# The second attention layer's scores as float32 products in two row halves, in place of float16 halves

## The reference, cut to what matters

```python
# layer 0: 8 channels for f and g
f = xf @ wf + bf;  g = xf @ wg + bg;  hh = xf @ wh + bh
s = einsum('bnk,bmk->bnm', g, f)
x = gamma * softmax(s, axis=-1) @ hh + x

# layer 1: 64 channels for q, k and v
q = x @ Wq + bq;  k = x @ Wk + bk;  v = x @ Wv + bv
energy = einsum('bic,bjc->bij', q, k)          # 4096 x 4096, contraction over 64 channels
attn = softmax(energy, axis=-1)
out = einsum('bmn,bmc->bnc', attn, v)          # summed over the softmax's ROW index m
x = gamma * out + x
```

## Time and profile before

| what | value |
|---|---|
| median of three runs | 5068.23 us |
| the profiled execution | 5049.6 us, span 5047.8 us |
| TensorE (PE) busy | 4836.0 us, 96% |
| VectorE (DVE) busy | 3533.9 us, 70% |
| ScalarE (ACT) busy | 2755.7 us, 55% |
| GpSimd (POOL) busy | 1831.4 us, 36% |
| score products of layer 1 (L468, L469) | 4096 records, 800.4 and 790.3 us busy |
| value products of layer 1 (L480) | 4096 records, 1095.2 us busy |
| maximum (L880), bias (L883) | 1024 each, 1251.2 and 219.2 us busy |
| projection of q and k (L541) | 128 records, 111.9 us busy |

### The profile page before, as it was taken

One profiled execution on the slowest core, in us unless ns is written; L12 is line 12 of the kernel. 1 busy time (PEld: TensorE's weight loads), 2 busy tenths in 40 slices (PEclk: granted clock), 3 DMA queues, 4 the chain that ended last, 5 costly groups with the idle time before them and its releaser, 6 DMA issues.

```text
span 5047.8 us, 75059 instructions
## 1 busy us (share of the span) xinstructions
PE 4836.0 (96%) x21608; PEld 1511.7 (30%) x21608; DVE 3533.9 (70%) x6722; ACT 2755.7 (55%) x3752; POOL 1831.4 (36%) x821
## 2 busy tenths in 40 slices
PE   7999999999999999999999999999999999999999
PEld 3224222242222422233222422224222242222422
DVE  6566876678765787558866588665885568866687
ACT  2555655556555565546655466554664546655465
POOL 2772017710177003760037600475005740067300
PEclk6998999989999899998989989998998989999899
DMA  0000000000000000000000000000000000000000
GB/s 26 1 9 17 0 8 1 9 17 0 9 1 9 17 0 9 1 9 17 0 10 1 18 9 0 9 1 24 2 0 10 1 26 0 0 9 3 24 0 8
DMA packets 13506, 40.03 MB, mean 8 GB/s; under 512 B 2620, under 2 KB 2620, under 8 KB 10812
## 3 DMA queue, kind: packets, MB, share of 16 engines
q1 hardware_dynamic: 13244, 36.78, 2.4%
HBM read 19.99 MB, written 8.39 MB: 6 GB/s over the span
## 4 chain that ended last, share of the span: by engine, by line
PE 61%; DVE 24%; issue 11%; ACT 2%; DVEq 1%; SPq 0%; ACTq 0%; DMA 0%
PE sum_banks L401 20%; DVE chunk_max L880 15%; PE score_banks L383 10%; PE sum_banks L366 9%; PE score_banks L468 5%; PE score_banks L469 4%; PE sum_banks L480 3%; PE sum_banks L417 3%; PE score_banks L541 2%; PE score_banks L340 2%; DVE tile_max L727 2%; DVE exp_bias L883 2%; ACT e_whole L659 1%; DVE inv_sum L862 1%; PE score_banks L325 1%
## 5 line engine op out<-in xcount | busy, mean ns | idle before, releaser
L727 DVE TENSOR_REDUCE tile_max<-sum_banks 128x1 f32<-128x512 f32 (+1 forms) x2128 | 1363.4, 686 | 914.3 <-PE sum_banks L366 914.1
L292 POOL TENSOR_TENSOR e_sum<-e_sum,e_whole 128x1024 f32<-128x1024 f32 x704 | 1655.4, 2351 | 429.7 <-ACT e_whole L600 409.2
L600 ACT ACTIVATE e_whole<-score_banks,no_bias 128x1024 f32<-128x1024 f32 x1024 | 1141.4, 1115 | 1105.2 <-PE score_banks L383 1103.1
L659 ACT ACTIVATE e_whole<-score_banks,exp_bias,down 128x1024 f32<-128x1024 f32 x1024 | 1233.3, 1204 | 764.7 <-DVE exp_bias L883 764.7
L880 DVE TENSOR_REDUCE chunk_max<-score_banks 128x1 f32<-128x1024 f32 x1024 | 1251.2, 1222 | 227.1 <-PE score_banks L469 212.9
L401 PE MATMUL sum_banks<-e_whole,proj 128*64 128x512 f32 x4096 | 1109.2, 627 | 27.0 <-DVE att L769 27.0
L480 PE MATMUL sum_banks<-e_whole,v_scaled 128*64 128x512 f32 x4096 | 1095.2, 617 | 6.6 <-DVE v_scaled L870 6.6
L289 POOL TENSOR_TENSOR e_sum<-e_whole 128x1024 f32<-128x1024 f32 x32 | 75.2, 2349 | 2231.3 <-ACT e_whole L600 2231.3
L468 PE MATMUL score_banks<-k_high,q_split 128*128 128x512 f16 x2048 | 800.4, 391 | 70.7 <-ACT e_whole L659 38.8
L469 PE MATMUL score_banks<-k_low,q_split 128*128 128x512 f16 x2048 | 790.3, 386 | 0.0
L366 PE MATMUL sum_banks<-f_tr,g_tr 72*128 72x512 bf16 x2128 | 693.2, 400 | 30.6 <-DVE tile_max L727 15.8
(11 more groups left out here) (100 smaller groups left out, 2074.3 us busy)
## 6 DMA issues: line engine op xcount, KB each, us to landing
x_in<-in_x_dram SPq DMA_DIRECT2D x19, 1024.0 KB, 4.9
out_dram<-x_mid SPq DMA_DIRECT2D x32, 256.0 KB, 2.2
k_high<-k_high SPq DMA_DIRECT2D x32, 128.0 KB, 2.2
k_low<-k_low SPq DMA_DIRECT2D x32, 128.0 KB, 2.2
gammas<-in_L_conv_gamma_dram SPq DMA_DIRECT2D x2, 0.5 KB
w<-in_L_conv_wg_dram SPq DMA_DIRECT2D x1, 2.0 KB
w<-in_L_conv_bg_dram SPq DMA_DIRECT2D x1, 0.0 KB
w<-in_L_conv_wf_dram SPq DMA_DIRECT2D x1, 2.0 KB
```

The costliest lines, as they stand in the source:

```text
L292: nc.gpsimd.tensor_tensor(acc, acc, e_whole[:, i % U0, :], ALU.add).then_inc(e_added, 1)
L600: nc.scalar.activation(e_whole[:, i % U0, :].rearrange("p (a n) -> p a n", a=2), score_banks[:, 2 * (i % 2):2 * (i % 2) + 2, :], ACT.Exp, ...
L659: nc.scalar.activation(e_whole[:, u, :].rearrange("p (a n) -> p a n", a=2), score_banks[:, 2 * (u % 2):2 * (u % 2) + 2, :], ACT.Exp, bias= ...
L727: nc.vector.reduce_max(tile_max[:, blk, j:j + 1], sum_banks[:, (2 + j % banks) % 4, :], AX_X).then_inc(a_used, 1)
```

## The change

The scores of layer 1 are computed from q and k in float32. `q2` holds q twice, on partitions 0 to 63 and 64 to 127. `k2` holds k's even blocks of 512 columns on partitions 0 to 63 and its odd blocks on 64 to 127. A step then has two products: the one of `h` 0 takes partitions 0 to 63 of both operands and writes one bank, the one of `h` 1 takes partitions 64 to 127 and writes the other. Each contracts over 64 partitions and writes 128 rows of 512 scores.

The weights of q are loaded twice side by side, so that one projection product writes q in both halves of the partitions. k's projection is a product of its own for each block of 512 columns, with 64 output columns of the weights; the odd block's product writes partitions 64 to 127. ScalarE copies q out of PSUM, VectorE copies k. The bound, the scaled weights, the split into high and low parts and SP's copies are gone. The maximum is taken negated and serves as the bias itself. TensorE's loop of `steps1` is written out.

```diff
-        w1 = sb("w1", [C1, 2, C], F32)
+        w1 = sb("w1", [C1, 2, 2, C], F32)
...
-        q_split = sb("q_split", [P, N], F16)
-        k_high = sb("k_high", [P, N], F16)
-        k_low = sb("k_low", [P, N], F16)
+        q2 = sb("q2", [P, N], F32)
+        k2 = sb("k2", [P, N // 2], F32)
...
-                sp.dma_start(w1[0:C, k, :], w_).then_inc(w_in, 16)
-                sp.dma_start(w1[C:C1, k, :], b_.unsqueeze(0)).then_inc(w_in, 16)
+                for copy in range(2):
+                    sp.dma_start(w1[0:C, k, copy, :], w_).then_inc(w_in, 16)
+                    sp.dma_start(w1[C:C1, k, copy, :], b_.unsqueeze(0)).then_inc(w_in, 16)
...
-                for j in range(NCH):
-                    cols = slice(j * CH, (j + 1) * CH)
-                    for part, done in ((k_high, high_done), (k_low, low_done)):
-                        sp.wait_ge(done, 2 * (image * NQ + (j + 1) * (CH // BANK)))
-                        sp.dma_start(part[0:C, cols], part[C:P, cols]).then_inc(k_copied[j], 16)
...
                 for h in range(2):
-                    col = (u % NCH) * CH + h * BANK
-                    bank = score_banks[:, 2 * (u % 2) + h, :]
-                    nc.tensor.matmul(bank, q_split[:, ds(i * P, P)], k_high[:, col:col + BANK], start=True, stop=False)
-                    mm = nc.tensor.matmul(bank, q_split[:, ds(i * P, P)], k_low[:, col:col + BANK],
-                                          start=False, stop=True)
+                    rows = slice(h * C, (h + 1) * C)
+                    mm = nc.tensor.matmul(score_banks[:, 2 * (u % 2) + h, :], q2[rows, i * P:(i + 1) * P],
+                                          k2[rows, (u % NCH) * BANK:(u % NCH + 1) * BANK], start=True, stop=True)
...
-                    if r == NCH - 2:
-                        pe.wait_ge(bound_sent, image + 1)
-                        nc.tensor.matmul(sum_banks[:, 0, 0:1], bound_in[:, :].to_broadcast([C1, P]), ones[:, :],
-                                         start=True, stop=True).then_inc(bound_ps, 1)
-                pe.wait_ge(w1s_ready, image + 1)
...
-                for c in range(NQ):
-                    if c < 4:
-                        pe.wait_ge(v1_sb, image * NCH + c + 1)
+                for c in range(NQ // 2):
+                    if c < 2:
+                        pe.wait_ge(v1_sb, image * NCH + 2 * c + 2)
                     else:
-                        pe.wait_ge(low_done, 2 * (image * NQ + c - 3))
-                    nc.tensor.matmul(score_banks[:, c % 4, :], w1s[:, :], x_tr[:, c * BANK:(c + 1) * BANK],
-                                     start=True, stop=True).then_inc(qk_ps, 1)
+                        pe.wait_ge(q_act, image * NQ + 2 * c - 2)
+                    for odd in range(2):
+                        cols = slice((2 * c + odd) * BANK, (2 * c + odd + 1) * BANK)
+                        nc.tensor.matmul(score_banks[:, 2 * (c % 2) + odd, :],
+                                         w1[:, 0, :, :].rearrange("p a c -> p (a c)"), x_tr[:, cols],
+                                         start=True, stop=True).then_inc(q_ps, 1)
+                    for odd in range(2):
+                        cols = slice((2 * c + odd) * BANK, (2 * c + odd + 1) * BANK)
+                        mm = nc.tensor.matmul(sum_banks[odd * C:(odd + 1) * C, c, :], w1[:, 1, odd, :], x_tr[:, cols],
+                                              start=True, stop=True, skip_group_check=True)
+                    mm.then_inc(k_ps, 1)
...
-                steps1(0, True)
-                with pe.Fori(1, T // 2) as t:
-                    steps1(t, False)
+                for t in range(T // 2):
+                    steps1(t, t == 0)
...
-                    for dst, rows in ((q_split, slice(0, C)), (k_high, slice(C, P))):
-                        nc.scalar.copy(dst[rows, c * BANK:(c + 1) * BANK], score_banks[rows, c % 4, :]
-                                       ).then_inc(high_done, 1)
+                    nc.scalar.copy(q2[:, c * BANK:(c + 1) * BANK], score_banks[:, c % 4, :]).then_inc(q_act, 1)
...
-                                             ACT.Exp, bias=exp_bias[:, u:u + 1], scale=down[:, 0:1],
+                                             ACT.Exp, bias=neg_max[:, u // NCH, u % NCH:u % NCH + 1],
...
+                for c in range(NCH):
+                    dve.wait_ge(k_ps, image * NCH + c + 1)
+                    nc.vector.tensor_copy(k2[:, c * BANK:(c + 1) * BANK], sum_banks[:, c, :]).then_inc(k_dve, 1)
...
-                        chain.link(nc.vector.reduce_max(chunk_max[:, odd, j:j + 1],
-                                                        score_banks[:, 2 * (u % 2):2 * (u % 2) + 2, :]
-                                                        .rearrange("p a n -> p (a n)"), AX_X))
-                        nc.vector.tensor_scalar(exp_bias[:, u:u + 1], chunk_max[:, odd, j:j + 1], neg_down[:, 0:1],
-                                                None, ALU.mult).then_inc(bias_ready, 1)
+                        nc.vector.tensor_reduce(neg_max[:, odd, j:j + 1], score_banks[:, 2 * (u % 2):2 * (u % 2) + 2, :]
+                                                .rearrange("p a n -> p (a n)"), AX_X, ALU.max, negate=True
+                                                ).then_inc(bias_ready, 1)
```

More of the change, by code:

```diff
@@ L128, in attention_pair_kernel @@
         no_bias = sb("no_bias", [P, 1], F32)
-        bound = sb("bound", [P, 1], F32)
-        pow2 = sb("pow2", [P, 1], F32)
-        inv_pow2 = sb("inv_pow2", [P, 1], F32)
-        up = sb("up", [P, 1], F32)
-        down1 = sb("down1", [P, 1], F32)
-        down = sb("down", [P, 1], F32)
-        neg_down = sb("neg_down", [P, 1], F32)
-        chunk_max = sb("chunk_max", [P, 2, NCH], F32)
-        exp_bias = sb("exp_bias", [P, U1], F32)
-        row_max1 = sb("row_max1", [P, 2], F32)
-        below_max = sb("below_max", [P, 2, NCH], F32)
+        neg_max = sb("neg_max", [P, 2, NCH], F32)
+        neg_row1 = sb("neg_row1", [P, 2], F32)
         chunk_w = sb("chunk_w", [P, 2, NCH], F32)
@@ L158, in attention_pair_kernel @@
         att0_ready, x_mid_ready = sem("att0_ready"), sem("x_mid_ready")
-        bound_sent, bound_ps, w1s_ready = sem("bound_sent"), sem("bound_ps"), sem("w1s_ready")
         v1_ps, v1_sb = sem("v1_ps"), sem("v1_sb")
-        qk_ps, high_done, low_done = sem("qk_ps"), sem("high_done"), sem("low_done")
-        k_copied = [sem(f"k_copied_{j}") for j in range(NCH)]
+        q_ps, k_ps, q_act, k_dve = sem("q_ps"), sem("k_ps"), sem("q_act"), sem("k_dve")
         s_ready, bias_ready, exp1_done, pv1_done = sem("s_ready"), sem("bias_ready"), sem("exp1_done"), sem("pv1_done")
-        below_ready, chunk_w_ready, y_ready = sem("below_ready"), sem("chunk_w_ready"), sem("y_ready")
+        row_ready, chunk_w_ready, y_ready = sem("row_ready"), sem("chunk_w_ready"), sem("y_ready")
         dve_step = sem("dve_step")
@@ L171, in attention_pair_kernel @@
         block = ctx.enter_context(nc.Block())
-        N_W = 14
+        N_W = 18
         def wait_x_tr(eng, image, layer, r=RT - 1):
@@ L548, in steps1 @@
                         if first and u < 2:
-                            pe.wait_ge(low_done, 2 * ((image + 1) * NQ - 2 + 2 * u))
+                            pe.wait_ge(q_act, (image + 1) * NQ - 2 + 2 * u)
                         if first and u < NCH:
-                            pe.wait_ge(k_copied[u], 32 * (image + 1))
+                            pe.wait_ge(k_dve, image * NCH + u + 1)
                         scores1(image, t * 2 + u // NCH, t * U1 + u, u)
+                        if first and u == 1:
+                            pe.wait_ge(k_dve, (image + 1) * NCH)
                         if first and 0 < u <= NCH:
@@ L665, in steps1 @@
                             odd = u // NCH
[L666 to L668 removed]
+                            act.wait_ge(row_ready, image * T + t * 2 + odd + 1)
+                            nc.scalar.activation(chunk_w[:, odd, :], neg_max[:, odd, :], ACT.Exp, scale=-1.0,
+                                                 bias=neg_row1[:, odd:odd + 1]).then_inc(chunk_w_ready, 1)
                         if first and 0 < u <= NCH:
@@ L703, in _ @@
             nc.vector.memset(x_tr[C:C1, :], 1.0).then_inc(const_ready, 1)
-            nc.vector.memset(x_abs[C:C1, :], 1.0).then_inc(const_ready, 1)
             dve.wait_ge(w_in, 16 * N_W)
-            chain.link(nc.vector.tensor_reduce(w_row[:, :], w1[:, :, :], mybir.AxisListType.XY, ALU.add,
-                                               apply_absolute_value=True))
-            START = chain.n
+            START = 0
             LINK_PIECES, LINK_MAX, LINK_ATT = 2, 4, 2
-            LINK_BOUND, LINK_CHUNK, LINK_BELOW, LINK_W = 8, 1, 1, 3
-            LINK_BLOCK = NCH * LINK_CHUNK + LINK_BELOW + LINK_W
+            LINK_W = 3
+            LINK_BLOCK = LINK_W
             L0 = NCH * (LINK_MAX + LINK_ATT)
-            BETWEEN = LINK_PIECES + LINK_BOUND
+            BETWEEN = LINK_PIECES
```

(2 more changed lines are left out.)

45 lines of the change are left out of this document (8 added, 37 removed).

## The result

| | before | after |
|---|---|---|
| median of 12 runs each | 5059.14 us (5044.95 to 5079.21) | 5114.72 us (5085.24 to 5136.20) |
| the profiled execution | 5049.6 us, span 5047.8 | 5114.86 us, span 5113.1 |

The account below looks back on a forecast made before the run. It took TensorE to bound the kernel, with VectorE holding up some late steps. Terms 29 + 68 - 16 - 10 + 2 = +73 us, added to the median 5068.2, gave 5141 us, 1.4% slower; likeliest range 5105 to 5180.

Parts of the forecast that it names:

- Score block, 1.06: Main steps of layer 1: two overlapping float32 score products make the block 1.06 us, where it was 0.97.
- its 262 us: Score pairs: estimate from the skill page's packing figures, 1.11 a pair instead of 0.86, 262 us more in all.
- The exposed load, 0.11: Score block: the first float32 weight load after the turn from values to scores is not hidden and adds 0.11 us.
- rival of the loads: Score block: serial loads, floor 2.18, 5247 us, chance 0.11; or loads cheap as column halves', floor 2.02, 5093, chance 0.07.
- TensorE alone sets the main part: Main part of layer 1: steps of 2.07 us without late ones, 1987 against 1958.5, +29 us.
- The relief 58, the dearer block 87: Main part: late steps ending on VectorE give back 58 us; the longer score block takes 87.
- Projection +68 at 0.50: Projection of q and k: 13.8 becomes 22.3 us an image at granted clock 0.50, +68 us in eight images.
- the clock rises in the projection: Rival, projection of q and k: clock goes to 1.00, 22.3 becomes 11.8, whole 5057 us; chance 0.10.
- Bound and scaling -16: Before layer 1's steps: the wait for scaled weights (12.3) and the bound's product (3.4) go, -16 us.
- Start +2: Kernel start: four more weight loads on SP's queue ahead of TensorE's first instruction, +2 us.
- First seven steps -10: Steps ahead of layer 1's main part: 20.98 becomes about 19.7 an image, -10 us in eight, bounds -20 and +8.
- low clock in the main part: Rival, main part: all-float32 work stays at 1.2 GHz, steps of 3.7 us, whole about 6700 us; chance 0.03.

Follow-up runs that it names:

- e1: The changed kernel with both score products of a step reading the same row half, which changes what is computed; 7076.54 us, one run.
- e8: e7 with q and k from one product of 128 columns, copied to the halves by ScalarE and VectorE as in e4; 4923.32 us, ratio 0.9718.
- e3: The changed kernel with one small VectorE operation put back between each maximum and the exponential; 5125.36 us, ratio 1.0132 to the kernel before.
- e5: The kernel before, float16 products kept, without bound and power-of-two scaling, negated maximum as bias; 4966.57 us, ratio 0.9815.
- e4: The changed kernel with q and k from one product of 128 columns, ScalarE and VectorE copying them to the partition halves; 5034.81 us, ratio 0.9942.
- e6: The changed kernel with the projection of q and k reading 128 rows instead of 65, the added rows zeros; 5033.3 us, ratio 0.9947.
- e10: e8 with layer 0's score products also reading 128 rows instead of 75, the added rows zeros; 4873.01 us, ratio 0.9637.
- e7: The changed kernel with all projections from x_tr, of both layers, reading 128 rows, the added rows zeros; 4942.43 us, ratio 0.9761.

## Why the prediction was right, and where its sizes were off

The direction and the mechanism held. Its steps, in its own order:

- **Score block, 1.06: right.** Measured 1.06, and e1's 1.91 shows that the overlap hangs on the two halves. The overlap was taken over from column halves without a row to show it. The page "TensorE: Matmul & The Clock Gate" of the Trainium skill, Part 3 on packing, gives four row tiles 3.07 times one, and the estimate made from it was a pair of 1.11 (its 262 us should read 266, 0.26 x 1024). With that pair the block would have been 1.31. It is 1.06, so the trace disagrees with carrying the four tiles' loss over to two. The same Part 3 has tiles start 4 ns apart; it is 7 ns here.
- **The exposed load, 0.11: right.** The second record comes about 0.11 late behind loads of 128 columns, and 0.05 to 0.06 late in the value block of the same step, behind loads of 64. The two blocks differ by that half (1.059 and 1.010). It isn't the rows: in e8's projection, on 128 rows and with 128 columns loaded, the second record behind a pause comes 0.533 after the first as well. Neither rival of the loads happened: the block is 1.06, and not 1.17 (one load after the other) or 1.01 (as cheap as the column halves').
- **TensorE alone sets the main part: right.** No late steps; e3 shows that VectorE has slack. +22.9 against +29 is a slip of the sum and not of the step: it set 960 whole steps of 2.07 against 1958.5, which is 0.53 short of whole steps in each image (4.2 in all), and 2.07 stands for 2.068 (1.5).
- **The relief 58, the dearer block 87: right.** e5 separates them, 62 and 85. The forecast kept the exponential at 1.20; it fell to 1.11, so part of the relief may be ScalarE's.
- **Projection +68 at 0.50: right**, +69.1. e4 takes 68 of it back. The rival "the clock rises in the projection" did not happen. e6 shows what it would have needed. With TensorE busy for all of the 22.42 us on 65 rows the clock stayed at 0.50; busy on 128 rows, from the same 0.50, it went to 1.00. The Trainium skill's page "TensorE: Matmul & The Clock Gate", Part 1, says that activity releases the throttle; by that rule alone the 22.42 would have risen too, and the trace disagrees.
- **Bound and scaling -16: nearly**, -13.8. TensorE's idle time there went from 12.3 to nothing, as priced; its busy time fell by 1.5, where the bound's product was put at 3.4. **Start +2: right**, +2.0.
- **First seven steps -10: the term that was mis-sized.** It measured -32.6, outside its bounds of -20 and +8. The working priced the waits one by one and let the clock stand. The windows of the kernel before, in the image of the earlier trace rows, show what it missed (the row of each lists the engines' busy times, then the clock):

```profile
1073.00:1075.00 2.00, 2.00 (x14) 1.48 (x13) 1.49 (x3) 1.30 (x2) 0.00 (x0) 0.50 0.30 66
1075.00:1077.00 2.00, 2.00 (x20) 1.44 (x19) 1.44 (x4) 1.38 (x3) 0.00 (x0) 0.78 0.00 0
...
1083.00:1085.00 2.00, 1.01 (x4) 0.31 (x4) 1.90 (x7) 1.83 (x3) 0.00 (x0) 1.00 0.00 0
1085.00:1087.00 2.00, 0.53 (x3) 0.23 (x3) 1.79 (x4) 1.44 (x3) 0.00 (x0) 0.78 0.00 0
1087.00:1088.50 1.50, 1.50 (x5) 0.51 (x4) 0.08 (x1) 1.16 (x2) 0.00 (x0) 0.50 0.00 0
```

  And the same stage of the kernel after:

```profile
1086.50:1088.50 2.00, 2.00 (x11) 0.49 (x8) 1.38 (x2) 0.60 (x1) 0.00 (x0) 0.57 0.00 0
1088.50:1090.50 2.00, 2.00 (x22) 1.15 (x20) 1.74 (x3) 1.50 (x3) 0.00 (x0) 1.00 0.03 8
1090.50:1101.37 10.87, 9.25 (x72) 4.40 (x70) 9.52 (x15) 9.95 (x17) 0.00 (x0) 1.00 0.00 1
```

  Before, the clock rose some 7 us into the stage, and after 1083, while TensorE was mostly waiting for ScalarE's exponential (1.54 busy of 4.00), it fell back to 0.50. After, it rises about 3.7 us into the stage and stays. e5, which has the same VectorE relief but float16 products, takes 149.4, and e4 141.0. So 18 of the 32.6 come with the relief (and e3, which puts one VectorE operation back, loses 7), and the other 14 with the new projection and float32 steps, where no wait for k_low stands. How each of these splits into waits and clock isn't settled: the two go together.
- **Layer 0, +20.6: not in the forecast.** Its code is the same, and e4's took 2435.8, e3's 2467.6. By e10's windows it goes with how long the clock stands at 0.50, which differs from image to image, and from run to run too: of the twelve runs of the kernel after, the one of 5085 us had a mean granted clock of 0.948 and the one of 5136 us 0.938. Such differences can make the gap between the profiles' +65 and the ratio's +49, though in which stage each run had them is not seen. **The last stage, -5.3,** is less waiting: TensorE is busy for 77.4 us in it both before and after. Which wait got shorter was not looked at.

That the sum came near is in part luck: in the two profiled executions two misses cancel, layer 0 with 20.6 above and the first seven steps with 22.6 below.

The rival "low clock in the main part" (6700) did not happen in the changed kernel, but e1 shows that it was no fancy: with its score products on 64 rows the clock stayed at 0.50 for 672.6 us, although the value products between them are on 128. The changed kernel differs from it only in that its two halves take up all 128 rows together. The chance of 0.03 was too small for what the trace of before could exclude.

## What to carry to other kernels

When a relieved engine and a dearer one share a step, cost each against the other's floor: the relief of VectorE and ScalarE was worth 62 us by itself (e5), and once TensorE's block was 0.09 longer, most of VectorE's part could be put back without cost to the main part (e3). Look at the granted clock of every short stage by its own, before counting instructions: zero rows under the contraction brought three stages from a granted clock of 0.50 to 0.81 up to 1.00, which is 157 of the 172 us that e7 takes off the changed kernel, and the 172 are three times what the change had cost. To have an operand on both halves of the partitions, let otherwise idle engines copy it before TensorE computes it twice.

## What the runs showed of the hardware

- In the projection the granted clock went with the rows that the products read, at equal busy time. On 65 rows TensorE stayed at 0.50 for 22.4 us eight times over (after). With zeros in rows 65 to 127 the clock rose within the stage (e6) or never fell (e7, e8). In e1, with scores on 64 rows and values on 128 in turn, it stayed at 0.50 for 672.6 us. In layer 0, score products on 75 rows gave images of 286 to 304 us, and on 128 rows 284.7 to 287.1 (e10). But the rows alone don't fix it: the same main part of e1 ran at 1.00 throughout in the other five images, and v's products on 65 rows ran at a mean of 0.50 to 0.66 (after). What decides between the two levels is open.
- Two float32 products on different row halves, 64 rows and 128 columns each, start 0.007 us apart and overlap wholly: the pair's block took 1.06 us, and 1.91 on the same half (e1).
- A load that nothing hides cost by its columns: the second record came about 0.11 us late behind float32 loads of 128 columns, 0.05 to 0.06 late behind those of 64.
- The exponential over 1024 columns became shorter by 91 ns when its scale was no longer a tensor. Before, and after (count, busy us, mean ns, idle before):

```profile
L659 ACT ACTIVATE e_whole<-score_banks,exp_bias,down 128x1024 f32<-128x1024 f32 x1024 | 1233.3, 1204 | 764.7 <-DVE exp_bias L883 764.7
```

```profile
L635 ACT ACTIVATE e_whole<-score_banks,neg_max 128x1024 f32<-128x1024 f32 x1024 | 1140.0, 1113 | 844.5 <-DVE neg_max L835 844.1
```

  The Trainium skill's page "ScalarE: Activation LUTs", under "What ACT_TABLE_LOAD costs", says that each scale or bias read from a tensor adds about 93 ns; the trace agrees. The forecast had kept 1.20 for it.
